# First attention's opening: scores and maxima of three units bank by bank, a second bank for key tiles, GpSimd's long subtractions in four pieces

## What is computed

```
x = x + first_attention(layernorm(x), ctx)   # 16 heads of 128
    q = (x @ Wq) / sqrt(128); k = ctx @ Wk; v = ctx @ Wv
    out = softmax(q k^T) v @ Wo
x = x + mixing(...) ; x = x + experts(...)
x = x + second_attention(layernorm(x), ctx)  # 16 heads of 16, q, k, v rounded to 8 bits
x = x + dilated_attention(...) ; x = x + feed_forward(...)
```

## Time and profile before

| | |
|---|---|
| median of three runs | 679.12 us (679.08 to 679.85) |
| profiled execution | 679.84 us, its span 678.5 us |
| TensorE products busy | 647.5 us, 95% |
| TensorE weight loads busy | 410.0 us, 60% |
| VectorE busy | 579.3 us, 85% |
| ScalarE busy | 412.9 us, 61% |
| GpSimd busy | 387.5 us, 57% |
| granted TensorE clock | full in every slice of the span |

### The profile page before, as it was taken

One profiled execution on the slowest core, in us unless ns is written; L12 is line 12 of the kernel. 1 busy time (PEld: TensorE's weight loads), 2 busy tenths in 40 slices (PEclk: granted clock), 3 DMA queues, 4 the chain that ended last, 5 costly groups with the idle time before them and its releaser, 6 DMA issues. The chain is left out here.

```text
span 678.5 us, 13895 instructions
## 1 busy us (share of the span) xinstructions
PE 647.5 (95%) x5089; PEld 410.0 (60%) x5089; DVE 579.3 (85%) x1038; ACT 412.9 (61%) x688; POOL 387.5 (57%) x499
## 2 busy tenths in 40 slices
PE   9899999999999999999999999998999989988897
PEld 7456676666676667677676657673456444544463
DVE  5998987897797898799989959888898899999865
ACT  4654455444455446556565433638998899899941
POOL 5886675656755655598986535345644643245401
PEclk9999999999999999999999999999999999999999
DMA  9656799757657678989976765779998999999910
GB/s 305 167 136 138 148 186 182 161 129 161 132 119 160 141 162 190 237 169 216 169 176 140 199 139 136 139 191 193 189 199 155 173 151 201 167 181 179 187 35 9
DMA packets 347827, 111.01 MB, mean 164 GB/s; under 512 B 313704, under 2 KB 344432, under 8 KB 347760
## 3 DMA queue, kind: packets, MB, share of 16 engines
q1 hardware_dynamic: 347760, 110.13, 78.7%
HBM read 31.97 MB, written 0.26 MB: 48 GB/s over the span
## 5 line engine op out<-in xcount | busy, mean ns | idle before, releaser
L1062 PE MATMUL psum<-c_nat,eT 128*128 128x256 f16 x1536 | 188.1, 273 | 0.9 <-ACT u_sb L1236 0.9
L1915 DVE TENSOR_REDUCE tops<-psum 128x1 f32<-128x512 f32 x256 | 158.8, 681 | 14.4 <-PE psum L1865 13.7
L1034 PE MATMUL psum<-cT,qk 128*128 128x512 f16 x744 | 165.6, 379 | 0.1
L1908 ACT ACTIVATE cT<-psum,bias,q_scale 128x1024 f16<-128x1024 f32 x128 | 153.4, 1204 | 16.9 <-PE psum L1865 16.1
L1062 PEld LDWEIGHTS psum<-c_nat,eT 128*128 128x128 f16 x1536 | 147.3, 98 | 24.1 <-issue 1.6
L1865 PE MATMUL psum<-kT,v_space 128*128 128x512 f16 x512 | 137.1, 380 | 10.7 <-DVE tops L1915 7.4
L1034 PEld LDWEIGHTS psum<-cT,qk 128*128 128x128 f16 x744 | 72.6, 98 | 82.3 <-issue 1.2
L1274 DVE TENSOR_REDUCE neg_max<-psum 128x1 f32<-128x2048 f32 x32 | 73.2, 2286 | 20.8 <-PE psum L1034 20.6
L1865 PEld LDWEIGHTS psum<-kT,v_space 128*128 128x128 f16 x512 | 44.5, 97 | 72.2 <-DVE tops L1915 36.1
L1262 DVE TENSOR_TENSOR e_lo<-e_all,e_hi 128x2048 f16<-128x2048 f32 x32 | 87.8, 2745 | 0.0
L1205 ACT ACTIVATE e_all<-psum,neg_max 128x2048 f32<-128x2048 f32 x32 | 63.0, 1970 | 16.7 <-DVE neg_max L1276 16.7
(11 more groups left out here) (289 smaller groups left out, 963.5 us busy)
## 6 DMA issues: line engine op xcount, KB each, us to landing
wvo_h<-in_L_xattn_Wv SPq DMA_DIRECT2D x30, 128.0 KB, 2.5
wvo_h<-in_L_xattn_Wo SPq DMA_DIRECT2D x30, 128.0 KB, 2.4
wqk_h<-in_L_xattn_Wq SPq DMA_DIRECT2D x28, 128.0 KB, 2.4
wqk_h<-in_wkT SPq DMA_DIRECT2D x28, 128.0 KB, 2.6
mx_land<-in_mx_weights SPq DMA_DIRECT2D x8, 384.0 KB, 4.0
v_space<-in_ctx SPq DMA_DIRECT2D x4, 512.0 KB, 5.9
cT<-in_ctx SPq DMA_DIRECT2D x2, 1024.0 KB, 8.1
c_nat<-in_expert_wT SPq DMA_DIRECT2D x2, 1024.0 KB, 6.3
```

Source lines behind the costliest of these rows:

```text
L1034: ins = pe.matmul(s_ps[:, n * 512:(n + 1) * 512], c.qk[:, u % 2, q_part, k, :], m.cT[:, b, c_part, 4 * n:4 * n + 4, k, :], start=(k, q_par ...
L1062: ins = pe.matmul(u_ps, c.eT[:, v % 2, e_part, j, :], m.c_nat[:, v // H0, c_part, j, :], start=(j, e_part, c_part) == (0, 0, 0), stop=(j, ...
L1908: act.activation(m.y[:, u % 2, q * CHUNK:(q + 1) * CHUNK], m.bank(second_place(u, q), 2), ACT.Exp, bias=m.bias[:, u:u + 1], scale=m.q_scal ...
L1915: dve.tensor_reduce(m.tops[:, n // NB, n % NB:n % NB + 1], m.bank(n % 3), AX.X, ALU.max, negate=True).then_inc(s["q_max"], 1)
```

## The change

Three edits. First, for units 0 to 2 (BY_BANK = 3) the scores are made bank by bank and each bank signals on its own. VectorE reduces each bank (`dve_bank_top`, 512 columns) into one of four columns of `part_max`, and takes the minimum of the four (they are negated maxima). In unit 0 the first two of these reductions stand in the setup, behind the split of h = 6 and behind dve_fold_key(1). The counts that others wait for follow from `scored(u)` and `limit_ready(u)`. Second, key tiles 1 and 3 (SPARE_KEYS) use bank 7, which attend needs only from u = 2 on; tile 1 waits for none before it, tiles 2 and 3 wait for the one before the last, tile 4 and later as before. Third, GpSimd's subtraction of 2048 columns is four instructions of 512 (LATE_PIECE = 2 tiles), of which the last signals.

```diff
--- before.py
+++ after.py
@@ -46,6 +46,9 @@
 AHEAD_PARTS = 4
 HALVED = TURNED - 1
 SPLIT = 6
+BY_BANK = 3
+SPARE_KEYS = (1, 3)
+LATE_PIECE = 2
 FIRST_PAIR = SPLIT - 4
 EARLY = ((0, 1), (1, 1), (0, 2), (1, 2), (1, 3), (1, 4))
 
@@ -312,6 +315,7 @@
         self.neg_max = sb("neg_max", [P, 2])
         self.row_sum = sb("row_sum", [P, UNITS])
         self.inv_sum = sb("inv_sum", [P, 1])
+        self.part_max = sb("part_max", [P, 4])
         self.wkv_land = flat(self.e_all)[:, 0:KD * 2 * D].rearrange("p (k n) -> p k n", k=KD)
         self.c_land = m.v_raw[:, KTB:KT, :]
         self.late_land = flat(m.cT[:, 1]).bitcast(F32).rearrange("p (t d) -> p t d", d=D)
@@ -762,10 +766,12 @@
                                ALU.subtract).then_inc(s["wqk_lo"], 1)
         side.upto(4 * u + 1)
         if u in (1, 2):
-            tiles = slice((u - 1) * LATE, u * LATE)
             pool.wait_ge(s["late_hi"], u)
-            pool.tensor_tensor(m.c_nat[:, 1, 1, tiles, :], c.late_land[:, tiles, :], m.c_nat[:, 1, 0, tiles, :],
-                               ALU.subtract).then_inc(s["late_lo"], 1)
+            for n in range((u - 1) * LATE, u * LATE, LATE_PIECE):
+                tiles = slice(n, n + LATE_PIECE)
+                ins = pool.tensor_tensor(m.c_nat[:, 1, 1, tiles, :], c.late_land[:, tiles, :], m.c_nat[:, 1, 0, tiles, :],
+                                         ALU.subtract)
+            ins.then_inc(s["late_lo"], 1)
         for kt in (2 * u, 2 * u + 1) if u < H0 else ():
             ints = d.k_int[:, kt % 2, :].rearrange("p (h d) -> p h d", h=H1)
             scale = spread(d.k_scale[:, kt % 2, :], 2, HD1)
@@ -875,7 +881,7 @@
 def act_fold_key(act, m, c, s, u):
     act.wait_ge(s["qk_mm"], u + 1)
     if u > 1:
-        act.wait_ge(s["scores"], u - 1)
+        act.wait_ge(s["scores"], scored(u - 2))
     act.copy(flat(c.qk[:, u % 2, 0]), m.bank(4)[:, P:3 * P]).then_inc(s["qk_hi"], 1)
 
 
@@ -899,15 +905,15 @@
     pe_fold_key(pe, m, c, d, s, 0, 0)
     pe_turn_context(pe, m, c, s, 2)
     pe_turn_context(pe, m, c, s, 3)
-    pe_first_scores(pe, m, c, s, 0)
+    pe_first_scores(pe, m, c, s, 0).then_inc(s["scores"], 1)
     pe_turn_context(pe, m, c, s, 4)
     pe_turn_context(pe, m, c, s, 5)
-    pe_first_scores(pe, m, c, s, 1)
+    pe_first_scores(pe, m, c, s, 1).then_inc(s["scores"], 1)
     pe_query(pe, m, c, d, s, 1)
     pe_turn_context(pe, m, c, s, 6)
     pe_turn_context(pe, m, c, s, 7)
     pe_fold_key(pe, m, c, d, s, 1, 1)
-    pe_first_scores(pe, m, c, s, 2)
+    pe_first_scores(pe, m, c, s, 2).then_inc(s["scores"], 1)
     pe_first_scores(pe, m, c, s, 3).then_inc(s["scores"], 1)
     pe.wait_ge(s["ln1"], NORM_STEPS * NORM["cross"])
     pe_turn_batch(pe, m, m.xn[:, 1, :], m.bank(6)).then_inc(s["xnT_mm"], 1)
@@ -989,7 +995,10 @@
     dve_fold_key(dve, m, c, s, 0)
     for h in range(2, 2 * GROUPS):
         turned(h)
+        if h == 2 * GROUPS - 2:
+            dve_bank_top(dve, m, c, s, 0, 0)
     dve_fold_key(dve, m, c, s, 1)
+    dve_bank_top(dve, m, c, s, 0, 1)
     dve.wait_ge(s["wkv_hi"], 1)
     dve.scalar_tensor_tensor(d.wkv[1][:, :, :], c.wkv_land[:, :, :], UP, d.wkv[0][:, :, :],
                              ALU.mult, ALU.subtract).then_inc(s["wkv_lo"], 1)
@@ -1017,6 +1026,16 @@
 def last_due(u):
 
     return u - 3 if TURNED <= u - 3 < UNITS else None
+
+
+def scored(u):
+
+    return u + 1 + 3 * min(u + 1, BY_BANK)
+
+
+def limit_ready(u):
+
+    return 2 * (u + 1) + 4 * min(u + 1, BY_BANK)
 
 
 def pe_cross(pe, m, c, d, g, s, side):
@@ -1028,6 +1047,15 @@
             pe.wait_ge(s["late_turned"], 32 * GROUPS)
         pe.wait_ge(s["qk_lo"], u + 1)
         pe.wait_ge(s["exp"], u)
+        if u < BY_BANK:
+            for n in range(4):
+                for k in range(KD):
+                    for q_part, c_part in TERMS:
+                        ins = pe.matmul(m.bank(n), c.qk[:, u % 2, q_part, k, :], m.cT[:, b, c_part, 4 * n:4 * n + 4, k, :],
+                                        start=(k, q_part, c_part) == (0, 0, 0),
+                                        stop=(k, q_part, c_part) == (KD - 1, 1, 0))
+                ins.then_inc(s["scores"], 1)
+            return
         for k in range(KD):
             for q_part, c_part in TERMS:
                 for n in range(4):
@@ -1039,13 +1067,15 @@
     def keys_values(kt):
         if kt == 0:
             pe.wait_ge(s["wkv_lo"], 1)
-        else:
+        elif kt > SPARE_KEYS[-1]:
             pe.wait_ge(s["k_biased"], kt)
+        elif kt > 1:
+            pe.wait_ge(s["k_biased"], kt - 1)
         if kt == KTB:
             pe.wait_ge(s["late_turned"], 32 * GROUPS)
         for k in range(KD):
             for w_part, c_part in TERMS:
-                ins = pe.matmul(kv_ps, m.cT[:, kt // KTB, c_part, kt % KTB, k, :], d.wkv[w_part][:, k, :],
+                ins = pe.matmul(key_bank(m, kt), m.cT[:, kt // KTB, c_part, kt % KTB, k, :], d.wkv[w_part][:, k, :],
                                 start=(k, w_part, c_part) == (0, 0, 0), stop=(k, w_part, c_part) == (KD - 1, 1, 0))
         ins.then_inc(s["kv"], 1)
 
@@ -1197,7 +1227,7 @@
         if w is not None:
             turned_out(w)
         if u < UNITS:
-            act.wait_ge(s["max"], 2 * u + 2)
+            act.wait_ge(s["max"], limit_ready(u))
             if u > 0:
                 act.wait_ge(s["e_lo"], u)
             else:
@@ -1268,11 +1298,19 @@
             remainder(u - 1)
         if u < UNITS:
             limit = c.neg_max[:, u % 2:u % 2 + 1]
-            dve.wait_ge(s["scores"], u + 1)
+            if u < BY_BANK:
+                for n in range(0 if u else 2, 4):
+                    dve_bank_top(dve, m, c, s, u, n)
+            else:
+                dve.wait_ge(s["scores"], scored(u))
             if u > 1:
                 dve.wait_ge(s["exp"], u - 1)
-            dve.tensor_reduce(limit, s_ps, AX.X, ALU.max, negate=True).then_inc(s["max"], 1)
-            dve.wait_ge(s["max"], 2 * u + 1)
+            if u < BY_BANK:
+                dve.wait_ge(s["max"], limit_ready(u) - 2)
+                dve.tensor_reduce(limit, c.part_max[:, :], AX.X, ALU.min).then_inc(s["max"], 1)
+            else:
+                dve.tensor_reduce(limit, s_ps, AX.X, ALU.max, negate=True).then_inc(s["max"], 1)
+            dve.wait_ge(s["max"], limit_ready(u) - 1)
             dve.tensor_scalar(limit, limit, 1.0 / UP, float(np.log(E_UP)), ALU.mult, ALU.add).then_inc(s["max"], 1)
         if 0 <= v < UNITS:
             if v > 0:
@@ -1317,8 +1355,20 @@
             add_output(last)
 
 
+def key_bank(m, kt):
+
+    return m.bank(7 if kt in SPARE_KEYS else 5)
+
+
+def dve_bank_top(dve, m, c, s, u, n):
+    dve.wait_ge(s["scores"], 4 * u + n + 1)
+    if u > 0 and n == 0:
+        dve.wait_ge(s["max"], limit_ready(u - 1))
+    dve.tensor_reduce(c.part_max[:, n:n + 1], m.bank(n), AX.X, ALU.max, negate=True).then_inc(s["max"], 1)
+
+
 def dve_key_tile(dve, m, d, s, kt):
-    ps, v_tile = m.bank(5), m.v_raw[:, kt, :]
+    ps, v_tile = key_bank(m, kt), m.v_raw[:, kt, :]
     heads = d.k_tmp.rearrange("p (h d) -> p h d", h=H1)
     dve.wait_ge(s["kv"], kt + 1)
     dve.scalar_tensor_tensor(v_tile, ps[:, D:2 * D], 1.0 / UP, d.bkv[:, D:2 * D], ALU.mult, ALU.add).then_inc(
@@ -1420,7 +1470,7 @@
 
 def dve_value_inverses(dve, m, s, ps):
     dve.wait_ge(s["v_scale_pe"], V_SCALE_PE["inverse"])
-    dve.wait_ge(s["scores"], H0)
+    dve.wait_ge(s["scores"], scored(H0 - 1))
     dve.tensor_copy(m.mix["v_inv"], ps[:, 0:D]).then_inc(s["v_scale_dve"], 1)
 
 
```

## The result

The changed kernel takes 683.07 us (median of six, 682.15 to 683.46), the kernel before beside it 679.37 (679.08 to 679.85): a ratio of 1.005, 95% interval 1.0039 to 1.006. That is outside the predicted range, on the slow side. The profiled execution took 683.18 with a span of 681.2.

What follows compares the result with a forecast made beforehand. It took TensorE, gapless from 77 to 350 us, as the bound, with 3.19 us of opening holes as ceiling. Pieces' savings paid for the 0.39 us split, leaving 0.15 us off the 679.12 median: 679.0 us, range 678.0 to 679.9.

Steps and rivals of the forecast that it cites:

- Unit 0: Opening, first unit: split maximum costs 0.39 us, two vanished VectorE waits give back 0.18 and 0.15; exp(0) net +0.06.
- The rule I had quoted for L1333: VectorE's and GpSimd's shared port: the loser blocks for the other's whole instruction; two-SBUF-input operations contend, tensor_reduce never.
- Rival 4: TensorE's clock halves at a 2.0 us hole before score(2), which then takes some 10.5 us: 684 us; chance 0.04.
- Unit 1: Second unit's maximum: splitting hides nothing and costs 0.39 us, exp(1) going from 31.28 to 31.67; gain capped at 0.51.
- The spare bank: Key tiles 1 and 3 go earlier, but TensorE then waits for the exponential; first two holes move, none closes: 0.
- The pieces: GpSimd's subtraction cut up at key tile 2: one 2.82 us VectorE stall becomes three summing to 2.2 to 2.4 us.
- Rival 1: Pieces free VectorE wholly, no short operation behind L1333 meets another: gain 0.51 us, time 678.6; chance 0.14.
- Rival 2: All three TensorE holes in the opening close: gain 3.19 us, time 675.9; chance 0.03.
- Rival 3: Later part: one e_lo subtraction meeting with GpSimd fewer or more gives 677.7 or 680.3, two 676.4 or 681.6; chance 0.17.
- my sum: Whole kernel: 679.84 us profiled, 1.34 of it around the span, less a gain of 0.15; from the median, 679.0 us.

Runs made afterwards that it cites:

- wkv_first: The changed kernel with VectorE's weight (wkv) subtraction issued before the first two bank tops in the setup, not between them: 0.1% slower than the kernel before.
- dve_tops: The kernel before with only VectorE's half of the bank edit, four bank reductions and a minimum where one reduction stood: 0.56 us slower by the medians.
- after_again: The changed kernel run once more, nothing altered: its profiled execution kept its clock, restart 1.21 us sooner; mean clock below 1.000 in one of five executions.
- in_hole: The changed kernel with unit 0's first two bank tops moved behind the split of h = 5, where VectorE idles: 681.7 us.
- in_hole_filled: in_hole with 45 unused products filling TensorE's hole before score(2): restart 1.14 us sooner than in_hole; total time not given in the text.

## Why the prediction was wrong

**The step that failed** is in "Unit 0". I pushed the weight subtraction back by two bank tops, counted for it only what it gained (0.18 us of waiting), and forgot to ask whom it now meets. The same paragraph has GpSimd's L736 starting at 17.88, and by its own terms the subtraction starts at 17.92. It has two inputs in SBUF, e_all and wkv. The price was 1.94 us. Taken off, exp(0) would be 7.52 - 1.94 = 5.58 after S, +0.06, the very number forecast. So the arithmetic held and a neighbour was missed that starts 0.04 us earlier, in the forecast's own terms as in the trace. The range of 678.0 to 679.9 had no room for it because no rival named it. The rule I had quoted for L1333 covers this case: the Trainium skill ("SBUF — State Buffer", "Who interferes with whom") also says that issue order and not the shape of the operation decides who blocks. The runs agree: 1.23 us when VectorE starts 0.98 ahead, 3.17 when it starts 0.04 behind.

**Rival 4, the clock,** had the right place and length (2.0 us forecast, 1.99 measured), and came true in part of the executions. The length is partly luck: it was worked out without the late weight subtraction, and wkv_first, which lacks that, has 1.92 and no fall in eleven. Two sizes were off. I priced the whole of score(2) at half clock (+5.2 us); eight of 24 products were (+1.69), and fold_key(3) covers 0.48 of that, so 1.21 is left. Its chance, 0.04, was too small for a length that the profile did not bound. The Trainium skill ("TensorE: Matmul & The Clock Gate", Part 1) has an idle engine throttled to half its clock; the runs agree: by the mean clock it fell in all six executions with a hole of 3.12 us, and in some with 1.99.

**Unit 1** held: +0.39 forecast for a split maximum. dve_tops shows exp(0) 0.39 later, and wkv_first exp(1) 0.41. **The spare bank** moved holes and closed none, as forecast; but with the bank tops it makes 1.77 us of idle TensorE into 1.99, and it is at 1.99 that a fall was seen. **The pieces** held in kind, three waits in a row; 2.2 to 2.4 us was forecast for their sum, 2.47 measured here and in wkv_first, 2.85 alone. Rival 1, VectorE freed wholly, did not happen. wkv_first, the kernel nearest to the one I had pictured, restarts 0.04 ahead of before (0 to 0.22 forecast). Rival 2 did not happen. Rival 3, a meeting more or less in the later part, doesn't show in the changed kernel: from restart to end it takes 0.2 us more than before, no more than the wait near 250 explains.

**Not in the prediction at all:** +0.36 us near 250 and +0.64 outside the span, where my sum kept the 1.34 as it was. The first and a good half of the second come with VectorE's bank tops, in a way that stays open. They are why wkv_first, its restart ahead of before, is still 0.7 us slower.

**Shares of the +3.7 us** between the medians: the meeting on VectorE and GpSimd 1.8 (wkv_first against after_again), the clock 1.2 where it falls (in_hole against in_hole_filled for the cause, after_again for the size), the two outer places 1.0 together, measured but not explained. They sum to 4.0, since the clock did not fall in every execution.

## What to carry to other kernels

When an instruction with two SBUF inputs moves, hold its new start against GpSimd's timeline. Here 0.98 us ahead cost nothing, and 0.04 us behind meant waiting out nearly the whole of the other's instruction. Before cutting up a long GpSimd instruction, try issuing it behind the short work: the pieces meet the next steps one by one and gave 0.04 us of the restart, the reordering 0.90, though neither made the whole kernel surely faster. And work moved from before a wait of TensorE's to an earlier place lengthens the idle stretch (1.77 to 1.99 us here), which can be enough for its clock to fall.

## What the runs showed of the hardware

- A VectorE operation with two SBUF inputs waited for the one GpSimd instruction that it met: 3.17 us against 1.23 beside 1024-column instructions, 2.21 beside 512-column ones. GpSimd lost time too: 5.20 us for its pair instead of 4.32.
- Beside back-to-back GpSimd pieces three VectorE instructions each waited for a piece: 0.64, 0.80 and 1.03 us. The reciprocal between the first two took its usual 0.25.
- TensorE's clock, 2.4 GHz through holes up to 1.54 us in the kernel before, fell to 1.2 GHz at a hole of 1.99 us in one profiled execution of a program and not in another; with a hole of 3.12 us the mean clock was below 1.000 in all six executions, with 1.92 us in none of eleven. After the fall eight products of 512 columns ran at 0.43 us each.
- An instruction of VectorE that waits for nothing can start late (0.28 us, and 0.22 with twelve memsets ahead), at a place that moved or vanished with the number of instructions before it (12, 26).
- Time outside the span differs between kernels by up to 0.8 us (1.3 to 2.1), and has to be added to any account made from a trace.
